# Attention scores for two heads at a time in the row halves of TensorE

## The reference

```python
xn = _layernorm(x, axis=-1)
x = x + _L0_attn_ref(xn, ...) + _L0_ffn_ref(xn, ...)
# attention: 16 heads of width 8, 256 tokens, rotary embedding on q and k
scores = jnp.einsum('bhtd,bhsd->bhts', q, k) / math.sqrt(D)
probs = jax.nn.softmax(scores, axis=-1)
attn = jnp.einsum('bhts,bhsd->bhtd', probs, v)
# mixture of experts: 16 experts of width 64, the best 2 per token, and one shared expert
hg = jnp.einsum('bsd,edi->bsei', x, experts_wg)
hu = jnp.einsum('bsd,edi->bsei', x, experts_wu)
all_outputs = jnp.einsum('bsei,eid->bsed', jax.nn.silu(hg) * hu, experts_wd)
return x + _mlp(x, shared_wg, shared_wu, shared_wd) + expert_weighted
```

## Time and profile before

| | |
|---|---|
| three runs | 251.49, 251.86, 252.37 us; median 251.86 |
| profiled execution | 251.57 us, span 249.8 us, so 1.8 us lie outside the span |
| granted TensorE clock | 0.963 of full speed on average, 0.58 between 20 and 40 us |
| busy share of the span | PE 86%, DVE 75%, POOL 69%, ACT 57% |

### The profile page before, as it was taken

One profiled execution on the slowest core, in us unless ns is written; L12 is line 12 of the kernel. 1 busy time (PEld: TensorE's weight loads), 2 busy tenths in 40 slices (PEclk: granted clock), 3 DMA queues, 4 the chain that ended last, 5 costly groups with the idle time before them and its releaser, 6 DMA issues.

```text
span 249.8 us, 4841 instructions
## 1 busy us (share of the span) xinstructions
PE 215.1 (86%) x1612; PEld 140.1 (56%) x1612; DVE 186.4 (75%) x400; ACT 141.6 (57%) x266; POOL 173.0 (69%) x247
## 2 busy tenths in 40 slices
PE   0473399997898999999858999999999999999973
PEld 0341165564555666676634566676767656675541
DVE  5885929999787687899935787998688878774301
ACT  2455033235556856675267567656666757667761
POOL 9186646899966748979195768778876774558622
PEclk9995559999999999999999999999999999999999
DMA  6925628120354331320744070504553540211201
GB/s 221 368 40 164 204 63 203 36 76 12 111 173 128 109 96 53 107 45 20 217 143 140 3 192 5 145 0 134 155 147 106 171 133 22 85 53 37 86 3 42
DMA packets 35953, 26.53 MB, mean 106 GB/s; under 512 B 4236, under 2 KB 30156, under 8 KB 35916
## 3 DMA queue, kind: packets, MB, share of 16 engines
q1 hardware_dynamic: 35224, 25.30, 34.8%
q10 hardware_dynamic: 704, 0.92, 1.0%
HBM read 18.53 MB, written 7.47 MB: 104 GB/s over the span
## 4 chain that ended last, share of the span: by engine, by line
PE 48%; DVE 21%; POOL 11%; issue 6%; DMA 5%; ACT 4%; SPq 4%; POOLq 0%; DVEq 0%; ACTq 0%
PE PV L514 8%; DVE mx L886 5%; PE S2b L500 4%; PE S2a L500 3%; PE S1a L486 3%; PE S1b L486 3%; PE Y L373 3%; PE FB L373 3%; SPq L302 3%; PE FA L373 3%; DMA wbc<-route_w 3%; POOL hid_lo L1001 2%; PE FA L375 2%; PE FA L374 2%; PE FB L375 2%
## 5 line engine op out<-in xcount | busy, mean ns | idle before, releaser
L1001 POOL TENSOR_TENSOR hid_lo<-gu,hid_hi 128x512 fp32r<-128x512 f32 (+1 forms) x36 | 46.4, 1288 | 26.6 <-ACT hid_hi L694 26.6
L661 ACT ACTIVATE probs<-S2b 128x512 f32<-128x512 f32 x64 | 38.1, 596 | 28.3 <-PE S2b L500 28.2
L985 POOL TENSOR_TENSOR gu<-gu,wbc 128x512 f32<-128x512 f32 x32 | 41.0, 1282 | 13.2 <-DMA wbc<-route_w 9.6
L886 DVE TENSOR_REDUCE mx<-S1a 128x2 f32<-128x512 f32 x65 | 44.4, 683 | 7.3 <-PE S1a L486 7.3
L886 DVE TENSOR_REDUCE mx<-S1b 128x2 f32<-128x512 f32 x63 | 43.0, 683 | 7.3 <-PE S1b L486 7.2
L661 ACT ACTIVATE probs<-S2a 128x512 f32<-128x512 f32 x64 | 38.3, 599 | 11.7 <-PE S2a L500 9.6
L514 PE MATMUL PV<-probs,vx 128*32 128x256 f32 x512 | 34.9, 384 | 4.3 <-ACT probs L661 4.3
L694 ACT ACTIVATE hid_hi<-gu 128x512 fp32r<-128x512 f32 (+1 forms) x36 | 22.7, 632 | 24.6 <-POOL gu L985 23.1
L895 DVE SCALAR_TENSOR_TENSOR th<-th,FA 128x512 f32<-128x512 f32 (+1 forms) x36 | 24.5, 682 | 13.7 <-ACT th L673 13.2
L673 ACT ACTIVATE th<-FA 128x512 f32<-128x512 f32 (+1 forms) x36 | 21.5, 597 | 18.5 <-PE FA L375 18.2
L876 DVE TENSOR_TENSOR gu<-FB,th 128x512 f32<-128x512 f32 (+1 forms) x36 | 24.6, 683 | 5.5 <-PE FB L375 5.4
(11 more groups left out here) (129 smaller groups left out, 433.1 us busy)
## 6 DMA issues: line engine op xcount, KB each, us to landing
wbc<-route_w SPq DMA_DIRECT2D x64, 128.0 KB, 3.1
q_hat<-q_parts SPq DMA_DIRECT2D x32, 96.0 KB, 2.8
k_hat<-k_parts SPq DMA_DIRECT2D x32, 96.0 KB, 2.7
k_parts<-parts SPq DMA_DIRECT2D x8, 192.0 KB, 2.2
q_parts<-parts SPq DMA_DIRECT2D x8, 192.0 KB, 2.2
x_sb<-in_x SPq DMA_DIRECT2D x4, 256.0 KB, 4.0
q_parts<-parts SPq DMA_DIRECT2D x8, 128.0 KB, 2.1
k_parts<-parts SPq DMA_DIRECT2D x8, 128.0 KB, 2.1
```

Of the source, the lines that this page charges most:

```text
L661: nc.scalar.activation(probs[:, head % (2 * NQ), :], S2[head % 2][:], ACT.Exp, scale=SCALE).then_inc(exp_done, 1)
L886: nc.vector.tensor_reduce(mx[:, (q // QB) % 2, (q // 2) % 2, :, q % 2, i], S1[use % 2][:].rearrange("p (t s) -> p t s", t=SB), axis=AX.X, ...
L985: nc.gpsimd.tensor_tensor(gu[:, m % 2, :], gu[:, m % 2, :], wbc[:, g % 2, c - 1, :], ALU.mult).then_inc(gu_weighted, 1)
L1001: nc.gpsimd.tensor_tensor(hid_lo[0:rows, m % 2, :], gu[0:rows, m % 2, :], hid_hi[0:rows, m % 2, :].bitcast(f32), ALU.subtract).then_inc(hi ...
```

## The change

Heads of a pair now lie at rows 0 to 47 and 64 to 111, with the three rows of their maxima right behind (48 to 50 and 112 to 114). `k_hat` has no zeros and one copy, so both memsets are gone. Two neighbouring heads of a quarter, one in each row half (`row_half`), run as a quad: four matmuls that alternate between the halves and between the two banks. A quad waits for both banks. On PE the scores stand in slots 0 and 2 alone, exponential quad, maximum quad, and behind those of slot 0 the values' matmuls and then hg. The transposing of the maxima moves from behind hg of the next block to the end of its own block. On DVE `th` comes after the second reduction, on ACT `hid_hi` moves from slot 2 to the end of slot 3 and tanh behind the second exponential, on POOL `hid_lo` of a chunk moves past the negation of the next block, and on SP the loads of routing weights stand at the head of a block, in front of `load_hats`, `load_max` and `scratch`. The maxima go by two DMAs of three rows instead of one of six.

```diff
-MROW = 2 * KROWS
+HROWS = 64
+KALL = KROWS + PARTS
...
+def row_half(q, i):
+
+    return (q + i) % 2
...
-            if i == 0 and transposed_half(blk) is not None:
-                s["M", transposed_half(blk)] = len(s)
+            if i == 3 and negated_half(blk) is not None:
+                s["M", negated_half(blk)] = len(s)
...
-                bank = take_s(("max", q * NQ + i))
+                banks = [take_s(("max", q * NQ + i)) for i in (first, first + 1)]
                 for t in range(SB):
...
+                    for i, bank in zip((first, first + 1), banks):
+                        r = row_half(q, i)
+                        rows, pair = slice(HROWS * r, HROWS * r + KROWS), NQ * hg + i
+                        last = nc.tensor.matmul(bank[:, t * T:(t + 1) * T], q_hat[rows, slot, pair, t * P:(t + 1) * P],
+                                                k_hat[rows, slot, pair, :], start=True, stop=True)
+                        if t == SB - 1:
+                            last.then_inc(s1_ready, 1)
...
                 if head >= 2:
-                    pe.wait_ge(exp_done, head - 1)
+                    pe.wait_ge(exp_done, head)
...
                 for i in range(NQ):
-                    if i == 1 and 0 <= blk - 1 < NBLK:
-                        attend(blk - 1)
                     if i == 2:
                         for kind, g in early_b(blk):
                             fill_b(kind, g)
+                    if i % 2 == 0:
+                        if 0 <= blk < NBLK:
+                            exp_scores(blk, i)
+                        if 0 <= q < NBLK:
+                            max_scores(q, i)
+                    if i == 0 and 0 <= blk - 1 < NBLK:
+                        attend(blk - 1)
...
+                    if i == 3 and negated_half(blk) is not None:
+                        maxima_to_rows(negated_half(blk))
...
-                    if i == 2 and 0 <= n - 1 < NCHUNKS:
+                    if i == 3 and 0 <= n - 1 < NCHUNKS:
...
-            nc.vector.memset(k_hat[0:MROW, 0].rearrange("p a r t -> p (a r t)").bitcast(u32), 0).then_inc(hat_zeroed, 1)
...
-                    if i == 0 and n < NCHUNKS:
+                    if i == 1 and n < NCHUNKS:
...
             for blk in range(FIRST, LAST + 1):
+                ahead = blk + CHLEAD + ROUTE_AHEAD
+                if 2 < ahead < NCHUNKS and ahead % NCH:
+                    load_route(ahead // NCH, ahead % NCH - 1)
                 if blk % 2 == 0 and blk // 2 + 3 in range(4, 2 * B):
                     load_hats(blk // 2 + 3)
...
                 if negated_half(blk) is not None:
                     negate_maxima(negated_half(blk))
+                if 0 <= m - 1 < NCHUNKS:
+                    rows = I if (m - 1) % NCH == 0 else P
+                    pool.wait_ge(hid_hi_ready, m)
+                    nc.gpsimd.tensor_tensor(hid_lo[0:rows, (m - 1) % 2, :], gu[0:rows, (m - 1) % 2, :],
+                                            hid_hi[0:rows, (m - 1) % 2, :].bitcast(f32), ALU.subtract).then_inc(hid_ready, 1)
```

More of the change, by code:

```diff
@@ L285, in _ @@
             for s in range(2):
-                sp.dma_start(k_hat[MROW:KALL, s], kones).then_inc(ld_kones, 16)
+                for r in range(2):
+                    sp.dma_start(k_hat[HROWS * r + KROWS:HROWS * r + KALL, s], kones).then_inc(ld_kones, 16)
             sp.dma_start(wout_sb[:], wout).then_inc(ld_wout, 16)
@@ L323, in load_max @@
                 half = h % 2
-                sp.dma_start(q_hat[MROW:KALL, (h // 2) % 2, NQ * half:NQ * (half + 1), :],
-                             mT[0:MROWS * NQ, h % 2, :]).then_inc(max_ld[h % 4], 16)
+                for r in range(2):
+                    sp.dma_start(q_hat[HROWS * r + KROWS:HROWS * r + KALL, (h // 2) % 2, NQ * half:NQ * (half + 1), :],
+                                 mT[PARTS * NQ * r:PARTS * NQ * (r + 1), h % 2, :]).then_inc(max_ld[h % 4], 16)
             def load_route(g, c):
@@ L477, in maxima_to_rows, with max_scores @@
                 last.then_inc(s1_ready, 1)
[L479 to L482, removed]
+            def max_scores(q, first):
+                b, hg, slot = q // QB, (q // 2) % 2, (q // QB) % 2
+                if q % 2 == 0 and first == 0:
                     pe.wait_ge(hat_ld[(q // 2) % 4], 64 * (q // 8 + 1))
-                bank = take_s(("max", q * NQ + i))
+                banks = [take_s(("max", q * NQ + i)) for i in (first, first + 1)]
@@ L495, in exp_scores @@
+            def exp_scores(q, first):
+                b, hg, slot, head = q // QB, (q // 2) % 2, (q // QB) % 2, q * NQ + first
+                if q % 2 == 0 and first == 0:
+                    pe.wait_ge(max_ld[(q // 2) % 4], 32 * (q // 8 + 1))
                     if q == 0:
-                        pe.wait_ge(ld_kones, 32)
+                        pe.wait_ge(ld_kones, 64)
                 if head >= 2:
-                    pe.wait_ge(exp_done, head - 1)
+                    pe.wait_ge(exp_done, head)
@@ L499, in exp_scores @@
                 for s in range(SB):
[L500 to L503, removed]
+                    for i in (first, first + 1):
+                        r = row_half(q, i)
+                        rows, pair = slice(HROWS * r, HROWS * r + KALL), NQ * hg + i
+                        last = nc.tensor.matmul(S2[i % 2][:, s * T:(s + 1) * T],
+                                                k_hat[rows, slot, pair, s * P:(s + 1) * P],
+                                                q_hat[rows, slot, pair, :], start=True, stop=True)
+                        if s == SB - 1:
+                            last.then_inc(s2_ready, 1)
@@ L666, in _ @@
                 for i in range(NQ):
+                    if 0 <= blk < NBLK:
+                        exponentials(blk * NQ + i)
                     if i == 1 and n < NCHUNKS:
@@ L997, in _ @@
                         split_batch(w, g, slot)
-                if 0 <= m < NCHUNKS:
-                    rows = I if m % NCH == 0 else P
-                    pool.wait_ge(hid_hi_ready, m + 1)
-                    nc.gpsimd.tensor_tensor(hid_lo[0:rows, m % 2, :], gu[0:rows, m % 2, :],
-                                            hid_hi[0:rows, m % 2, :].bitcast(f32), ALU.subtract).then_inc(hid_ready, 1)
                 for kind, g in early_b(blk):
@@ L1040 @@
     cos, sin = rope_tables()
-    kones = np.zeros((MROWS, H // 2, 2, T), np.float32)
-    for r in range(2):
-        kones[PARTS * r:PARTS * (r + 1), :, r] = 1.0
+    kones = np.ones((PARTS, H // 2, T), np.float32)
     bf = mybir.dt.np(mybir.dt.bfloat16)
```

61 lines of the change are left out of this document (18 added, 43 removed).

## The result

| | before | after |
|---|---|---|
| median, us (runs) | 251.49 (251.26 to 252.37, 7 runs) | 254.70 (253.31 to 256.50, 7 runs) |
| ratio after / before | | 1.0122 (95%: 1.0086 to 1.0159) |
| profiled execution, us | 251.57 | 255.34 |
| its span, us; mean granted clock of TensorE | 249.8; 0.963 | 253.5; 0.942 |

The kernel became slower by 1.2%, where 240.7 us had been forecast. First the page of after: busy time by engine, the granted clock in 40 slices, and the shares of the chain that ended last; they answer to the earlier trace rows.

What follows compares the result with a forecast made beforehand. PE's list was taken to set the pace of most of the middle. Middle -10.5, POOL +0.8 and end -1.2 took 251.6 to 240.7 us; the forecast's own range was 236 to 245, the full range 231 to 251.5.

Steps and rivals of the forecast that it cites:

- The rest: Small changes on POOL, SP and memsets, including the negation ahead of `hid_lo` (2.6 against 2.7 us): counted as nothing.
- Down waits behind the negation: Rival: PE's down waits for `hid_lo`, late by 1.35 us in fifteen even blocks; +20 us, 261; chance 0.05.
- Quad 0.25: On PE, four score matmuls in two row halves were to take 0.25 us, with 0.46 if halves don't overlap.
- turn 0.10: On PE, each switch between matmul shapes was to cost 0.10 us; three more turns a block, counted as 0.40.
- the loop: From DVE's last reduction through quad, values, hg, tanh and `th` to the next reductions: 4.89 us, plus 0.28 every second block.
- the routing loads: On SP, loads moved ahead of the scratch writes were to remove POOL's 4.76 us wait for routing weights.
- PE's list and the end: PE's blocks were to shrink from 4.99 to 4.80 us, and the last four blocks to save 1.2 us.
- +0.8 for POOL's splits: On POOL, blocks with neighbouring splits were to run 0.4 over PE's 5.98 us in seven blocks, adding 0.8 us.
- sum of the new PE block: PE's values 1.00, quads 1.00, three projections 2.30 and turns 0.50 were to make 4.80 us; light blocks 5.13.
- Loop and extras add up: Rival: extra projections lengthen the loop, light blocks 5.03 + 0.33 and heavy 5.03 + 1.18 us; 246.8 us; chance 0.17.

Runs made afterwards that it cites:

- e4: The changed kernel with the exponential quad of slot 2 run nine times over in blocks 0, 12 and 28, writing the same values again; 251.90 us.
- e6: The kernel before with only SP's routing loads moved ahead of `load_hats`, `load_max` and `scratch`; 247.10 us.
- e10: e7 with the routing loads moved back to the end of SP's block; 247.91 us.
- e2: The changed kernel with POOL's `hid_lo` ahead of the negation and O2's add moved behind the next block's `hid_lo`; 245.09 us.
- e9: e7 with scores at full width (96 or 102 rows with zeros) and the maxima by one DMA, order of all lists kept; 250.59 us.
- e7: e2 with the values' matmuls moved behind hg; 243.77 us.
- e11: e6 with POOL's `hid_lo` moved behind the next block's negation, and so behind O2's add; 254.95 us.
- e5: e2 with the four matmuls of every quad written head by head (a, a, b, b); 245.24 us.

## Why the prediction was wrong

**The step that failed** is "The rest", in the words "Nothing for these". The prediction saw that the negation now stands ahead of `hid_lo`, weighed 2.6 against 2.7 us, and called it "hidden, just". Three things were wrong in it.

- It started both sides of the race at the end of the last reduction, so it took POOL to be free at that instant. Where that was so, the race came out as worked out: behind the eight negations that waited for the maxima PE waited once, for 0.39 us. In the other eight POOL came later than the maxima, and there `hid_lo` is late by what POOL is late and by the negation's 1.4 us on top: six waits, 8.7 us.
- It did not ask what POOL does ahead of the negation. That is O2's add with its own wait (4.00 us at the worst place), past which `hid_lo` was moved as well, and `xT_lo` (3.48 us) or a split, which had stood ahead of `hid_lo` before too, but without the negation behind them.
- It had no price for what an idle PE does to its clock; to be rid of that was worth 2.8 us (e4).

Measured, the step that was put at 0 costs 7.9 us in the old kernel and 9.6 in the new one (7.1 and 9.7 by ratios). The rival that names it ("Down waits behind the negation") had the mechanism, but a chance of 0.05 against POOL's 18 us of idle time. That was the wrong witness: POOL was idle, for 20.4 us ahead of negations alone, but nearly always in other blocks than those in which PE waited. Idle time of an engine in total says nothing of where it lies.

**What was right.** Quad 0.25 forecast, 0.23 measured; turn 0.10, measured 0.10; the loop 5.17 for a block with the copy, measured 5.19 (in part by luck: PE's own list is 4.98 of it, with a transposing that the sum left out); the routing loads 4.8, measured 5.0 (e6) and 4.1 (e10). On the quads the Trainium skill ("TensorEngine Tiling (Array Packing)", Key Properties) says that independent tiles run in parallel and that a change of mode drains the array; the trace agrees, with 0.23 us for four matmuls in two halves and 0.10 for a turn.

**Other terms that were off.** The forecast for PE's list and the end came to 5.7 + 1.2 us beside the routing loads (18 x 0.19 + 12 x 0.19, and the last blocks). With POOL's order mended (e2) the kernel is 0.9736 of before, -6.6 us, of which the routing loads are 5.0; that leaves 1.6. The row halves brought about what had been forecast, 6.3 us (e9 to e7). What ate it is the new order around them, 3.2 us even at full width (e6 to e9), and the values ahead of hg, 1.6 more (e7 to e2); the forecast had nothing for either, and no run priced its +0.8 for POOL's splits. How the 3.2 us are shared between the banks' joint waits, the later transposing of the maxima and the rest was not tried. One piece of it is seen in the rows of after: from the last matmul of hu to the next quad it is 0.33 us, but with the transposing of the maxima between them 0.57 (209.17 to 209.74), in every second block. The sum of the new PE block has no term for that. It makes 0.12 us a block, and light blocks of after take 5.24 us from quarter 20 to 26 and not 5.13, about half way to the 5.36 of the rival "Loop and extras add up".

**Put together** in us, by ratios to 252: routing loads -5.1 (e6), the new order at full width +3.2 (e9), the row halves -6.3 (e7), the values ahead of hg +1.6 (e2), POOL's order +9.7 (after): +3.1. The steps were measured in this one order, and a part may be worth something else beside others, as POOL's order is: +7.1 in the old kernel (e11).

## What to carry to other kernels

An instruction that is moved back in an engine's list takes on the time and every wait of what it is moved past, up to the head of the list. List them with their waits at the places where extras meet, and don't settle it with an average of idle time. A margin that is counted from one event, as here from the last reduction, holds only where the engine is free at that event: ask in which blocks it comes late, and out of what. A stall of PE can cost more than its length, since the clock can fall behind it. When a large change disappoints, exchange single statements of the engines' lists before giving up its main idea: here two of them on POOL and one on PE turned +1.2% into -3.3%.

## What the runs showed of the hardware

Two things had not been expected. In e5 matmuls written a, a, b, b for two row halves started as a, b, a, b (204.94, 204.95, 205.06, 205.07), and their order in the program made no difference to the time (245.24 and 245.09 us). The Trainium skill ("TensorE: Matmul & The Clock Gate", Part 3) has matmuls start strictly in the program's order; these rows differ from it, at least as the profiler records the starts, and the measured time agrees with the rows.

And TensorE's clock fell in the middle of a busy kernel. In after PE waited for 1.5 to 3.1 us before 60.21, 137.34 and 230.92, and the granted clock then fell to 0.50. With matmuls that did nothing new in these gaps it stayed at 1.00 (e4). The length of a wait alone does not settle it: in e11 a wait of 1.57 us (before 61.12) was followed by such a stretch and one of 1.78 us (before 137.99) was not. And it is not tied to `hid_lo`: in e2 the clock also fell behind a wait of 1.92 us for DVE's maxima (before 58.28).
